# Attention inside a two-layer kernel: the four output turns of a unit as transposes with a permutation

## The reference, cut to what matters

```
def xattn(q, k, v):                      # q: layernorm(x); k = v: ctx, 4 x 512 x 128
    qh = q.reshape(B, S, KV, G, D).transpose(0, 2, 3, 1, 4)   # KV 8, G 4, D 16
    kh = k.reshape(B, S, KV, D).transpose(0, 2, 1, 3)
    vh = v.reshape(B, S, KV, D).transpose(0, 2, 1, 3)
    scores = jnp.einsum('bkgsd,bktd->bkgst', qh, kh) / sqrt(D)
    weights = softmax(scores, axis=-1)
    out = jnp.einsum('bkgst,bktd->bkgsd', weights, vh)
    return out.transpose(0, 3, 1, 2, 4).reshape(B, S, 512)
x = x + tanh(g_xattn[layer]) * xattn(layernorm(x), ctx, ctx)
```

## Time and profile before

| what | value |
|---|---|
| median of 3 runs (lowest, highest) | 2155.77 us (2149.66, 2156.09) |
| profiled execution: its own time, its span | 2151.34 us, 2149.6 us |
| PE busy | 1973.5 us, 92% of the span |
| DVE, ACT, POOL busy | 1325.7, 1105.8, 752.2 us |
| first and last start of L366 | 65.5 us, 1430.1 us |
| mean granted TensorE clock | 0.968 of full speed |

### The profile page before, as it was taken

How to read it: one execution, slowest core, us unless ns; L and a number is a source line. 1 busy time by engine, 2 the same in 40 slices (tenths; PEclk the granted TensorE clock), 3 DMA queues, 4 the chain that set the end, 5 groups by cost and what they waited for, 6 DMA issues and landing times. The chain is left out here.

```text
span 2149.6 us, 40775 instructions
## 1 busy us (share of the span) xinstructions
PE 1973.5 (92%) x10072; PEld 1222.5 (57%) x10073; DVE 1325.7 (62%) x2547; ACT 1105.8 (51%) x1801; POOL 752.2 (35%) x912
## 2 busy tenths in 40 slices
PE   5999999979999999993999999988789999999997
PEld 2444444334667658882434444433557888888886
DVE  7888888732234325533888888856776455555553
ACT  2777777832112115541577777763113566666664
POOL 3122222112201005554122222221664555565564
PEclk9999999989999999996799999999999999999998
DMA  5322222150000128765422222213005888888886
GB/s 162 88 60 63 56 64 62 29 217 19 1 0 1 69 83 197 169 111 123 132 70 56 56 60 66 56 49 107 0 5 174 190 187 198 200 204 205 202 196 103
DMA packets 96018, 219.90 MB, mean 102 GB/s; under 512 B 16930, under 2 KB 20004, under 8 KB 95908
## 3 DMA queue, kind: packets, MB, share of 16 engines
q1 hardware_dynamic: 61540, 138.80, 22.3%
q0 software_dynamic: 33792, 79.71, 19.1%
q10 hardware_dynamic: 576, 0.00, 0.0%
HBM read 114.64 MB, written 56.63 MB: 80 GB/s over the span
## 5 line engine op out<-in xcount | busy, mean ns | idle before, releaser
L597 DVE TENSOR_REDUCE maxima<-ring_ps 128x1 f32<-128x512 f32 x1024 | 644.8, 681 | 116.2 <-PE ring_ps L386 115.9
L491 ACT ACTIVATE probs<-score_ps 128x1024 f32<-128x1024 f32 x512 | 494.0, 1020 | 47.7 <-PE score_ps L403 45.3
L386 PE MATMUL ring_ps<-k_turned,q_turned 64*128 64x512 f32 x1024 | 407.6, 477 | 32.1 <-DMA q_turned<-q_lo 13.3
L1091 PE MATMUL bank_f<-w_gu_parts_f,xg_T_f 128*128 x1800 | 368.1, 353 | 2.0 <-issue 2.0
L386 PEld LDWEIGHTS ring_ps<-k_turned,q_turned 64*128 64x128 f32 x1024 | 176.9, 192 | 326.1 <-DVE maxima L597 205.8
L1091 PEld LDWEIGHTS bank_f<-w_gu_parts_f,xg_T_f 128*128 128x128 f32 x1800 | 326.6, 190 | 30.2 <-issue 2.6
L403 PE MATMUL score_ps<-q_turned,k_turned 64*128 64x512 f32 x1024 | 326.7, 450 | 14.7 <-ACT probs L491 14.3
L418 PE MATMUL out_ps<-probs,v_ones 128*32 128x512 f32 x2048 | 274.5, 608 | 0.8 <-ACT probs L491 0.7
L1116 PE MATMUL bank_f<-w_dn_parts_f,hg_T_f 96*128 (+1 forms) x888 | 242.6, 409 | 2.5 <-DVE hg_T_f L1653 1.4
L916 POOL DMA_INDIRECT out_x<-y_tok_f,idx_out_f x111 | 176.7, 1592 | 137.4 <-ACT y_tok_f L1291 104.9
L900 POOL DMA_INDIRECT xg_f<-xh_rows_f,idx_in_f x156 | 158.1, 1014 | 186.3 <-DVE idx_in_f L1543 114.5
(11 more groups left out here) (211 smaller groups left out, 2252.2 us busy)
## 6 DMA issues: line engine op xcount, KB each, us to landing
w_gu_f<-in_L_w_gu SPq DMA_DIRECT2D x64, 384.0 KB
q_turned<-q_hi SPq DMA_DIRECT2D x128, 128.0 KB, 2.6
w_dn_f<-in_L_w_dn SPq DMA_DIRECT2D x32, 384.0 KB
k_turned<-k_hi SPq DMA_DIRECT2D x128, 64.0 KB, 2.1
q_turned<-no_max SPq DMA_DIRECT2D x64, 128.0 KB, 2.6
q_turned<-q_lo SPq DMA_DIRECT2D x64, 128.0 KB, 2.6
xh_rows_f<-xh_f SPq DMA_DIRECT2D x8, 1024.0 KB, 9.0
w_gu_f<-in_L_w_gu SPq DMA_DIRECT2D x16, 512.0 KB
```

The lines of the kernel that those rows point to most:

```text
L386: pe.matmul(ring(k, "max", i), q_turned[rows, slot, h // 2, c * P:(c + 1) * P], k_turned[rows, slot, :], start=True, stop=True).then_inc(m ...
L491: act.activation(probs[:, c % 2, pair, :, :], score_ps[:, pair, :, :], ACT.Exp, scale=float(D) ** -0.5).then_inc(exped, 1)
L597: dve.tensor_reduce(maxima[:, par, col:col + 1], ring(k, "max", i), AX.X, ALU.max).then_inc(max_taken, 1)
L1091: mm = pe.matmul(bank[:, half, 0:2 * F], xg_T[:, half, x_part, d, :], w_gu_parts[:, bass.ds(par, 1), w_part, d, :].rearrange("p a f -> p ( ...
```

## The change

`pick` becomes a full 128 x 128 permutation: its first 68 columns are as before, and the 60 rows that were not picked get the columns behind them (a second `affine_select` on POOL). `turn_out` issues four transposes with `pick` in the place of the identity instead of four fp32 matmuls. A transpose writes 128 columns, of which 68 are wanted. Block c still starts at column c * 68, so it overwrites the 60 unwanted columns of block c - 1. Only the last block's unwanted columns remain, and the turned maxima move behind them, from column 272 to `MAX_AT` = 332.

```
--- before.py
+++ after.py
@@ -30,6 +30,8 @@
 AHEAD = 4
 
 USED = D + 1
+HEAD_ROWS = P // G
+MAX_AT = (TPB - 1) * G * USED + P
 TURN_AT, TURN_Q_AT, INVERT_AT = 2, 5, 8
 COPY_OUT_AT, COPY_TURN_AT, COPY_Q_AT = 1, 3, 6
 
@@ -78,7 +80,7 @@
         maxima = sb("maxima", [P, 2, SLOTS])
         max_parts = sb("max_parts", [P, 2, 2 * SLOTS], F32R)
         max_rows = sb("max_rows", [2 * SLOTS, 2, P], F32R)
-        pick = sb("pick", [P, G, USED])
+        pick = sb("pick", [P, P])
         probs = sb("probs", [P, 2, 2, 2, S])
         out_rows = sb("out_rows", [P, S])
         recip, turned_out = sb("recip", [P, SLOTS]), sb("turned_out", [P, SLOTS * USED])
@@ -212,8 +214,12 @@
             pool.memset(v_ones[:, :, :, D:D + 1], 1.0).then_inc(pool_set, 1)
             pool.memset(pick[:], 0.0).then_inc(picked, 1)
             pool.wait_ge(picked, 1)
-            pool.affine_select(out=pick[:], in_=pick[:], compare_op=ALU.not_equal, fill=1.0, base=0,
-                               pattern=[[-P // G, G], [-1, USED]], channel_multiplier=1).then_inc(picked, 1)
+            used_first = pick[:, 0:G * USED].rearrange("p (h e) -> p h e", h=G)
+            pool.affine_select(out=used_first, in_=used_first, compare_op=ALU.not_equal, fill=1.0, base=0,
+                               pattern=[[-HEAD_ROWS, G], [-1, USED]], channel_multiplier=1).then_inc(picked, 1)
+            unused = pick[:, G * USED:P].rearrange("p (h e) -> p h e", h=G)
+            pool.affine_select(out=unused, in_=unused, compare_op=ALU.not_equal, fill=1.0, base=-USED,
+                               pattern=[[-HEAD_ROWS, G], [-1, HEAD_ROWS - USED]], channel_multiplier=1).then_inc(picked, 1)
             pool.wait_ge(pool_set, 3)
 
             def root(b, n=0):
@@ -351,7 +357,7 @@
                     return
                 pe.wait_ge(max_split, u + 1)
                 ring_bank_free(b, k, "turn")
-                pe.transpose(ring(k, "turn")[0:2 * SLOTS, SLOTS * USED:SLOTS * USED + P].bitcast(F32R),
+                pe.transpose(ring(k, "turn")[0:2 * SLOTS, MAX_AT:MAX_AT + P].bitcast(F32R),
                              max_parts[:, (k - LAG_NEG) % 2, :], ident_r[:]).then_inc(max_turned, 1)
 
             def turn_out(b, k):
@@ -361,10 +367,10 @@
                 if stage(b, k, LAG_NEG) is None:
                     ring_bank_free(b, k, "turn")
                 if isinstance(b, int) and u == 0:
-                    pe.wait_ge(picked, 2)
+                    pe.wait_ge(picked, 3)
                 for c in range(TPB):
-                    mm = pe.matmul(ring(k, "turn")[:, c * G * USED:(c + 1) * G * USED], out_rows[:, c * P:(c + 1) * P],
-                                   pick[:].rearrange("p h e -> p (h e)"), start=True, stop=True)
+
+                    mm = pe.transpose(ring(k, "turn")[:, c * G * USED:c * G * USED + P], out_rows[:, c * P:(c + 1) * P], pick[:])
                 mm.then_inc(out_turned, 1)
 
             def head_rows(a):
@@ -478,7 +484,7 @@
                 if past(b, k, LAG_NEG + 2):
 
                     act.wait_ge(max_placed[par], 16 * u + (0 if par == 0 else -16))
-                act.activation(max_rows[:, par, :], ring(k, "turn")[0:2 * SLOTS, SLOTS * USED:SLOTS * USED + P], ACT.Copy
+                act.activation(max_rows[:, par, :], ring(k, "turn")[0:2 * SLOTS, MAX_AT:MAX_AT + P], ACT.Copy
                                ).then_inc(max_copied, 1)
 
             def exp(b, k, c, pair):
```

## The result

| kernel | median | runs | range |
|---|---|---|---|
| before | 2153.35 us | 19 | 2145.42 to 2160.61 us |
| changed | 2147.69 us | 19 | 2141.35 to 2152.96 us |

The ratio, of the means of the runs (2147.2 and 2153.5 us), is 0.9971, with a 95% interval of 0.9961 to 0.9981: 6.2 us less, between 4.1 and 8.4. The sum had said 7.0.

The account below looks back on a forecast made before the run. Before m7, PE's turn and DVE's reduction of m5 were taken to arrive almost together; from m8 on, its issue sets the step. 4.4 + 2.6 = 7.0 us off the 2155.8 us median gave 2148.8 us, range 2139 to 2157.

Parts of the forecast that it names:

- The sum: Whole kernel: 4.4 us from clean steps plus 2.6 us from closing steps, 7.0 us less.
- The price of a turn: Output turn on PE: four transposes instead of eight fp32 instructions, 1.00 to 0.58 us, saving taken as 0.44 us.
- Clean steps: 44 steps with L386 matmuls and no DVE piece between m4's and m5's reductions: 0.10 us less each, 4.4 us.
- The 14 steps with extra work: Steps with a DVE piece in front of m5's reduction: m7 already waits for it, so a gain of 0.
- Closing steps: Last three steps of each layer, no L386 left, ACT idle before its copy: 6 x 0.44 = 2.6 us less.
- Full saving: Rival: PE is the bound, so each of 64 turns gives its whole 0.44 us, 28 us less; chance 0.07.
- No change to measure: Rival: transposes do not overlap or something else holds the step; only closing steps gain, 0 to 3 us; chance 0.14.
- Blocks that wait for each other: Rival: overlapping column writes make the turn's transposes go one after another, 1.32 us a turn, 16 us more; chance 0.06.
- The clock: Rival: turns without real matmuls lower PE's granted clock in each batch, some 46 us more, 2202 us; chance 0.03.
- a feed-forward part that changes by more than a few us: Sign against the forecast: feed-forward parts, which the change does not touch, moving by more than a few us.

Follow-up runs that it names:

- thrice: Changed kernel with every transpose of the output turn issued three times into the same columns; ratio 1.0092 to the kernel before.
- two_and_two: Changed kernel with blocks 0 and 1 turned by the old fp32 matmuls, blocks 2 and 3 by transposes; ratio 0.9972 to the kernel before.
- short_after: Changed kernel with the DVE reductions of m4 and m5 taken over 256 of the 512 keys; ratio 0.9831 to the kernel before.
- piece7_after: Changed kernel with the DVE work between the reductions of m4 and m5 moved behind that of m7; ratio 0.9934 to the kernel before.
- short: Kernel before and changed kernel, each with the reductions of m4 and m5 over 256 of 512 keys; ratios 0.9959 and 0.9831 to the kernel before.
- early: Kernel before and changed kernel, each with the turn moved from round 2 to round 1; ratios 1.0212 and 1.0073 to the kernel before.
- mid: Kernel before and changed kernel, each with the turn moved to between m4 and m5; ratios 1.0077 and 0.9957 to the kernel before.

## Why the prediction was right, point by point

**The price of a turn.** 1.00 to 0.58 us forecast, 0.55 measured, the saving 0.45 where I had taken 0.44. The rows of the query transposes were the right price, and neither the permutation nor the overlap of the blocks costs anything: in thrice, with three writes over the same columns, transposes still follow each other after 0.11 us.

**Clean steps: 0.10 us.** Measured 0.11 in the step, through the wait that was forecast (m7 for m5's reduction). two_and_two, thrice and short_after show that this wait, and nothing else, takes the rest of the saving. That no second path holds the shifted step was argued then, and short_after shows it.

**The 14 steps with extra work: 0.** Measured 0.01 or less in each of layer 0. The wait of m7 took the whole saving, and piece7_after shows that it was the piece in front of m5.

**Closing steps: 0.44 us each.** Measured 0.45.

**The sum.** 7.0 us forecast, 6.2 measured with an interval of 4.1 to 8.4. The stretch from first to last copy has 6.3 us of it in the two layers; the first copy's own shift of 0.44 a layer stands outside that stretch and belongs to no gain. 58 of the 64 turns lie in steps with a ring, and there 0.10 of 0.45 us, or nothing, counts. The level is partly luck: 2148.8 us was forecast from a median of three runs, 2155.8 us, and 2147.7 was measured, but the 19 runs put the kernel before at 2153.4 us, from where the same sum gives 2146.4.

**The rivals.** Full saving (28 us): excluded in this kernel by the step of 11.47 us, and real in three others, where the hold on m7 is away or the turn stands elsewhere (short, early and mid, 26 to 30 us). No change to measure: excluded by the interval. Blocks that wait for each other: excluded by the 0.11 us. The clock: 1.00 through the attention. One of the signs that were to prove the forecast wrong did turn up in the profile, a feed-forward part that changes by more than a few us: the 719.1 and 727.0 us above. The eleven other profiles, at 720.6 to 726.9 us with matmuls and with transposes alike, show it to be scatter. The Trainium skill says ("TensorE: Matmul & The Clock Gate", section "Part 4: PE-mode transpose") that transposes do not count as activity for the full clock; in thrice, with 12 of them in a step instead of 4, the granted clock is 1.00 from 60 to 440 us, and 0.968 over the whole profile, as before. So the rule changes nothing in these kernels, and no run here tells whether it holds.

**What I had wrong** lies in the experiments, not in the forecast: for a moved turn I forgot the turn's own bank and POOL's split of the maxima in one case, and split a pair of matmuls in the other.

## What to carry to other kernels

A stage whose engine is 92% busy can still give back only a fraction of what is saved in it, if at the next shared buffer another engine arrives just behind. Look for the first wait behind the edit, and see how late its other condition comes: here m5's bank, released just before m7's load at 387.67, while PE's own work kept m7's matmul until 387.87. That gap, 0.20 us, is the most that the edit can bring, and 0.10 of it was lost again, since m7 alone takes 0.43 us to the next group where in its pair it takes 0.33. If it is smaller than the saving, the better edit is on the other path, or both together: 6 and 9 us apart were 36 us together. And price an order by the buffer of the moved work itself and by the neighbours that ran beside it, not by the waits behind it alone.

## What the runs showed of the hardware

Two matmuls that each use 64 rows of the array ran side by side: the group of four took 0.67 us and the group of three, with one left alone, 0.66 us as well. Of fp32 work with the same 128-column stationary block, a matmul of 68 columns took two instructions 0.11 us apart, and a transpose of 128 columns one instruction of 0.11 us. A halved reduction (256 instead of 512 columns) on DVE cost 0.38 us instead of 0.65. And the untouched part of the same program differed by up to 8 us between profiled executions, which is more than the effect studied here.
